# A decoder layer on one core: PSUM banks picked by waits already paid, and the last of four evictions waits for the other engine

## The reference

```
x = x + nystrom_attention(N(x))       # 16 heads of 16, 64 landmarks, softmax kernels q k_l, q_l k_l, q_l k
x = x + cross_attention(N(x), ctx)    # 64 context rows, masked softmax
x = x + ffn(N(x))                     # 8 experts, one picked per batch by its last token; N(x) + 0.3 (..)
```

```
KV = X @ V
V  = 0.25 * V @ (13 I - KV @ (15 I - KV @ (7 I - KV)))
```

## Time and profile before

| | |
|---|---|
| median of three runs | 1399.54 us |
| the profiled execution, its own time | 1397.8 us |
| span of that profile, first to last instruction | 1396.1 us |
| TensorE busy | 1355.2 us, 97% |
| VectorE, ScalarE, GpSimd busy | 1029.5, 667.0, 571.1 us |

### The profile page before, as it was taken

How to read it: one execution, slowest core, us unless ns; L and a number is a source line. 1 busy time by engine, 2 the same in 40 slices (tenths; PEclk the granted TensorE clock), 3 DMA queues, 4 the chain that set the end, 5 groups by cost and what they waited for, 6 DMA issues and landing times.

```text
span 1396.1 us, 53472 instructions
## 1 busy us (share of the span) xinstructions
PE 1355.2 (97%) x23732; PEld 889.7 (64%) x23732; DVE 1029.5 (74%) x2194; ACT 667.0 (48%) x1230; POOL 571.1 (41%) x799
## 2 busy tenths in 40 slices
PE   6998999999999999999999999999999999999998
PEld 4756666666766767665666766666666656676555
DVE  3487887758786886878778686877868777898641
ACT  2424355454555546355554644555454544435652
POOL 6223444443626244362534436153353543417132
PEclk9999999999999999999999999999999999999999
DMA  8002010120201011020101101010110100001122
GB/s 285 1 3 95 3 63 3 45 75 3 66 5 51 20 38 33 3 66 5 51 20 37 34 3 58 13 51 20 37 34 3 52 2 19 18 4 39 25 77 65
DMA packets 40536, 53.18 MB, mean 38 GB/s; under 512 B 9698, under 2 KB 30450, under 8 KB 40306
## 3 DMA queue, kind: packets, MB, share of 16 engines
q1 hardware_dynamic: 31602, 41.37, 9.2%
q10 hardware_dynamic: 8704, 8.39, 1.8%
HBM read 37.16 MB, written 12.59 MB: 36 GB/s over the span
## 4 chain that ended last, share of the span: by engine, by line
PE 85%; DVE 5%; ACT 3%; issue 2%; POOL 1%; DMA 1%; DVEq 1%; POOLq 0%; SPq 0%; ACTq 0%
PE bank L1322 41%; PE bank L1575 8%; PE bank L1341 7%; PE bank L1331 7%; PE bank L1564 3%; PE bank L1530 2%; PE bank L1418 2%; PE bank L1397 2%; PE bank L1462 2%; PE bank L1543 2%; PE bank L1451 2%; ACT p3T L896 1%; PE bank L1385 1%; PE bank L1562 1%; PE bank L1424 1%
## 5 line engine op out<-in xcount | busy, mean ns | idle before, releaser
L778 POOL TENSOR_TENSOR b<-ut,eye 128x256 f32<-128x256 f32 x192 | 137.6, 733 | 498.6 <-DVE ut L1161 428.9
L940 ACT ACTIVATE az<-bank 128x320 f32<-128x320 f32 x192 | 67.5, 400 | 185.6 <-PE bank L1331 185.2
L1322 PE MATMUL bank<-xnT_a,wqkv 128*128 128x512 f32 x256 | 123.6, 609 | 0.3 <-ACT xnT_a L864 0.3
L1218 DVE RECIPROCAL oT_x<-bank 128x256 f32<-128x256 f32 x64 | 109.2, 1733 | 19.2 <-PE bank L1575 19.2
L1322 PE MATMUL bank<-w2e,hT 128*128 128x256 f32 x512 | 119.0, 386 | 1.5 <-ACT hT L1006 1.4
L1218 DVE RECIPROCAL oT<-bank 128x256 f32<-128x256 f32 x64 | 111.5, 1747 | 10.6 <-PE bank L1575 10.6
L1322 PE MATMUL bank<-xnT_c,w1e 128*128 128x512 f32 x256 | 117.0, 597 | 1.3 <-DVE m_x L1192 0.9
L1090 DVE TENSOR_REDUCE m<-bank 128x1 f32<-128x512 f32 x128 | 82.9, 680 | 38.5 <-PE bank L1418 36.9
L1322 PEld LDWEIGHTS bank<-w2e,hT 128*128 128x128 f32 x512 | 96.0, 192 | 16.9 <-issue 2.7
L896 ACT ACTIVATE p3T<-bank 128x512 f32<-128x512 f32 x128 | 66.7, 603 | 79.1 <-PE bank L1451 78.9
L959 ACT ACTIVATE pT_x<-bank,neg_bias 128x512 f32<-128x512 f32 x128 | 79.9, 696 | 29.8 <-PE bank L1564 28.8
(11 more groups left out here) (223 smaller groups left out, 2979.2 us busy)
## 6 DMA issues: line engine op xcount, KB each, us to landing
x_in<-in_x SPq DMA_DIRECT2D x16, 512.0 KB, 3.8
w1e<-in_W SPq DMA_DIRECT2D x16, 512.0 KB, 3.5
w2e<-w2o SPq DMA_DIRECT2D x16, 512.0 KB, 4.1
out<-base ACTq DMA_DIRECT2D x32, 256.0 KB, 2.1
row_e<-w2o_row SPq DMA_DIRECT2D x16, 128.0 KB, 4.6
hT<-in_W2T SPq DMA_DIRECT2D x2, 512.0 KB, 6.5
pT_x<-in_ctxT SPq DMA_DIRECT2D x1, 1024.0 KB
ctxT<-in_ctxT SPq DMA_DIRECT2D x16, 64.0 KB, 2.6
```

Source lines behind the costliest of these rows:

```text
L778: return g.tensor_tensor(b7[:, q, :], ut[:, q, :], eye[28 if it else 7][:].unsqueeze(1) .broadcast_to([P, 4, LM]), ALU.subtract).then_inc( ...
L1218: return v.reciprocal(oT[x][:, k, cols], tile(i, ("den" + x, k))[:, cols]).then_inc(dve_done, 1)
L1322: last = mm(dst, lhsT, rhs, start=(k == 0), stop=(k == len(pairs) - 1))
```

## The change

Three things are changed; the written order, the arithmetic and the instructions that compute are the same.

First, `plan()` looks at the first three free banks and not at the first alone. It keeps, for A and for D, the highest number that TensorE has waited for. A bank costs 0 if its emptying step is covered by that already, 1 if the step is of an engine that this P step waits for anyway, and 2 otherwise. The cheapest is taken, the oldest of equal ones. A table `operands(step)` lists the A and D steps that a P step needs. Second, of the four evictions of an inverse level, the one that comes last in the written order first waits for both evictions of the other engine. Third, TensorE's waits are asked for together (`counts`): a wait is left out where another engine's step that is waited for has itself waited for it (`reached`), and the remaining ones are issued in an order fixed for each kind.

```diff
+    waited = {"A": 0, "D": 0}
     for engine, i, step in PROGRAM:
...
         if engine == "P":
+            asked = set()
+            for who, name in operands(step):
+                if done[who, i, name] > waited[who]:
+                    waited[who] = done[who, i, name]
+                    asked.add(who)
             for j in range(banks_of(step)):
-                bank[i, step, j], before[i, step, j] = free.pop(0)
+                price = [0 if emptier is None or done[emptier] <= waited[emptier[0]] else
+                         1 if emptier[0] in asked else 2 for _, emptier in free[:3]]
+                bank[i, step, j], emptier = free.pop(price.index(min(price)))
+                before[i, step, j] = emptier
+                if emptier and done[emptier] > waited[emptier[0]]:
+                    waited[emptier[0]] = done[emptier]
+                    asked.add(emptier[0])
...
+def closes_half(engine, i, step):
+    mine = ORDER[engine, i, step]
+    return all(ORDER[key] <= mine for h in range(2) for key in (("D", i, ("wb", step[1], h)), ("A", i, ("az", step[1], h))))
...
+        def counts(eng, emptied, i, **steps):
+            need = {"A": emptied["A"], "D": emptied["D"], "G": 0}
+            for who, names in steps.items():
+                need[who] = max([need[who], *[DONE[who, i, s] for s in names]])
+            mine = passed.setdefault(eng, {})
+            need = {who: n for who, n in need.items() if n > mine.get(done[who], 0)}
+            left = {who: n for who, n in need.items()
+                    if not any(reached[other, m].get(done[who], 0) >= n for other, m in need.items())}
+            for who, n in left.items():
+                for sem_, m in (*reached[who, n].items(), (done[who], n)):
+                    mine[sem_] = max(mine.get(sem_, 0), m)
+            return {who: left.get(who, 0) for who in need.keys() | set("ADG")}
...
 # ScalarE, before the eviction az
+                    if closes_half("A", i, step):
+                        if c := unmet(act, "D", i, ("wb", it, 0), ("wb", it, 1)):
+                            act.wait_ge(dve_done, c)
...
 # VectorE, before the eviction wb
+                    if closes_half("D", i, step):
+                        if c := unmet(dve, "A", i, ("az", it, 0), ("az", it, 1)):
+                            dve.wait_ge(act_done, c)
...
 # TensorE, one kind of many
                 elif kind in ("jT", "jZ"):
-                    if c := due(pe, "D", emptied, i, ("wb", it, 0), ("wb", it, 1)):
-                        pe.wait_ge(dve_done, c)
-                    if c := due(pe, "A", emptied, i, ("az", it, 0), ("az", it, 1)):
-                        pe.wait_ge(act_done, c)
+                    c = counts(pe, emptied, i, A=[("az", it, 0), ("az", it, 1)], D=[("wb", it, 0), ("wb", it, 1)])
+                    if c["D"]:
+                        pe.wait_ge(dve_done, c["D"])
+                    if c["A"]:
+                        pe.wait_ge(act_done, c["A"])
```

More of the change, by code:

```diff
@@ L327, with operands @@
 PROGRAM = program()
+def operands(step):
+    kind, n = step[0], step[1] if len(step) > 1 else 0
+    if kind in ("q", "k", "v"):
+        return [("A", ("xnTa", 0)), ("A", ("xnTa", 1))]
+    if kind in ("xnTb", "xnTc"):
+        return [] if step == ("xnTb", 0) else [("A", ("nmB",) if kind == "xnTb" else ("nmC", n))]
+    if kind in ("s3", "s1", "sx"):
+        return [("A", ({"s3": "k", "s1": "q", "sx": "qx"}[kind], n))]
+    if kind in ("t1", "tx"):
+        return [("A", ("mT" + kind[1],))]
+    if kind in ("x2T", "mT3", "t3", "mT1", "mTx"):
+        return [("D", ({"x2T": "soft2", "mT3": "mp3", "t3": "mT3", "mT1": "mp1", "mTx": "mpx"}[kind],))]
+    if kind in ("zT", "den1", "denx", "o1", "ox"):
+        e = {"z": "e3", "d": "e" + kind[-1], "o": "e" + kind[-1]}[kind[0]]
+        return [("A", (e, n, j)) for j in range(4)]
+    if kind in ("z", "a", "qx", "gate", "logit", "h", "y3"):
+        names = {"z": [("zT", 0), ("zT", 1)], "a": [("x2T",)], "qx": [("xnTb", 0), ("xnTb", 1)], "gate": [("xnTc", 1)],
+                 "logit": [("gate",)], "h": [("xnTc", 0), ("xnTc", 1)], "y3": [("h", f) for f in range(4)]}[kind]
+        return [("A", name) for name in names]
+    if kind in ("iT", "iZ"):
+        if n == 0:
+            return [("A", ("a", 0)), ("A", ("a", 1))]
+        return [("D", (x, n - 1, h)) for x in (("uz",) if kind == "iT" else ("uz", "ut")) for h in range(2)]
+    if kind in ("jT", "jZ"):
+        return [(e, (x, n, h)) for e, x in (("D", "wb"), ("A", "az")) for h in range(2)]
+    if kind == "y":
+        return [("D", ("uz", ITERS - 1, 0)), ("D", ("uz", ITERS - 1, 1))]
+    if kind in ("w1", "wx"):
+        return [("D", ("o" + kind[1], 0)), ("D", ("o" + kind[1], 1))]
+    return []
 def plan():
@@ L504, in unmet, with run @@
             return n if first(eng, done[who], n) else 0
-        def due(eng, who, emptied, i, *steps):
-            n = max(emptied[who], *[DONE[who, i, s] for s in steps])
-            return n if first(eng, done[who], n) else 0
+        def counts(eng, emptied, i, **steps):
+            need = {"A": emptied["A"], "D": emptied["D"], "G": 0}
+            for who, names in steps.items():
+                need[who] = max([need[who], *[DONE[who, i, s] for s in names]])
+            mine = passed.setdefault(eng, {})
+            need = {who: n for who, n in need.items() if n > mine.get(done[who], 0)}
[5 more added lines that the diff above has]
+            return {who: left.get(who, 0) for who in need.keys() | set("ADG")}
         def tile(i, step, j=0):
             return banks[BANK[i, step, j]]
-        def run(who, body):
+        def run(who, eng, body):
             for engine, i, step in PROGRAM:
@@ L517, in run @@
                     body(i, step)
+                    if (who, i, step) in DONE:
+                        reached[who, DONE[who, i, step]] = dict(passed.get(eng, {}))
         def half(n):
@@ L1013, in body @@
                     return last.then_inc(act_done, 1)
-            run("A", body)
+            run("A", act, body)
         @block.vector
@@ L1374, in body @@
                         pe.wait_ge(ctx_loaded, 16 * (i + 1))
+                    c = counts(pe, emptied, i)
+                    if c["A"]:
+                        pe.wait_ge(act_done, c["A"])
+                    if c["D"]:
+                        pe.wait_ge(dve_done, c["D"])
                     for r in range(2):
@@ L1387, in body @@
                     x = kind[-1]
[L1388 to L1392, removed]
-                            pe.wait_ge(act_done, c)
+                    c = counts(pe, emptied, i, **({"G": [("lnB", 0)]} if (x, n) == ("b", 0) else {"A": [("nmB",) if x == "b" else ("nmC", n)]}))
+                    if c["D"]:
+                        pe.wait_ge(dve_done, c["D"])
+                    if c["A"]:
+                        pe.wait_ge(act_done, c["A"])
+                    if c["G"]:
+                        pe.wait_ge(pool_done, c["G"])
                     for k in range(KD):
@@ L1453, in body @@
                 elif kind == "zT":
[L1454 to L1457, removed]
+                    c = counts(pe, emptied, i, A=[("e3", n, j) for j in range(4)], D=[("v", 0), ("v", 1)])
+                    if c["D"]:
+                        pe.wait_ge(dve_done, c["D"])
+                    if c["A"]:
+                        pe.wait_ge(act_done, c["A"])
                     for h in range(2):
@@ L1605, in body @@
                         pe.wait_ge(expert_out_loaded, 32 * (i + 1))
-                    if c := due(pe, "A", emptied, i, *[("h", f) for f in range(FM)]):
-                        pe.wait_ge(act_done, c)
+                    c = counts(pe, emptied, i, A=[("h", f) for f in range(FM)])
+                    if c["D"]:
+                        pe.wait_ge(dve_done, c["D"])
+                    if c["A"]:
+                        pe.wait_ge(act_done, c["A"])
                     for t in range(2):
@@ L1620, in body @@
                     fuse_consts(pe)
+                    c = counts(pe, emptied, i)
+                    if c["A"]:
+                        pe.wait_ge(act_done, c["A"])
+                    if c["D"]:
+                        pe.wait_ge(dve_done, c["D"])
                     last = chain(o[0:EXPERTS, 0:D], [(b2T[:, k, :], wfo[:, k, :]) for k in range(KD)])
                 last.then_inc(pe_done, 1)
-            run("P", body)
+            run("P", pe, body)
 def kernel(**inputs):
```

242 lines of the change are left out of this document (149 added, 93 removed), and 3 rows, old and new, of the table OPERANDS_FROM.

## The result

The changed kernel took 1428.06 us (median of five executions, 1424.85 to 1431.53) against 1399.49 before: 28.6 us or 2.0% slower, ratio 1.0204 with a 95% interval of 1.0184 to 1.0224. A sixth execution, of 3806.4 us, was in a slow state and is left out; with it the median is 1428.89. Forecast were 1427 us in a range of 1409 to 1440. The profiled execution after took 1431.53 us with a span of 1429.8, so 33.7 us more span than before.

The account below looks back on a forecast made before the run. TensorE, 97% busy in a fixed order, was taken as the bound. Delays of 0.11 + 0.40 + 0.42 + 0.63 + 0.18 = 1.74 us a turn, times 16, gave 27.8 us and 1427 us; range 1409 to 1440.

Parts of the forecast that it names:

- middle turn: One repeat of the regular pattern, nine in all (batches 4 to 12); predicted 1.74 us later each.
- s1.1: TensorE step whose new bank is emptied by a ScalarE step ending at 710.28; predicted +0.11 us.
- iT.1: TensorE step at inverse level 1 whose new bank waits for VectorE's reciprocal of the batch before; predicted +0.40 us.
- jT.1: TensorE step at inverse level 1, behind a ScalarE eviction now held for VectorE's last one; predicted +0.42 us.
- t1.1: TensorE step whose new bank waits for ScalarE's first eviction of level 2, one step later; predicted +0.63 us.
- jZ.5: TensorE step at inverse level 5, behind a ScalarE eviction held for VectorE's; predicted +0.18 us.
- jT.2: TensorE step at inverse level 2; predicted no longer to wait for VectorE's eviction, with the turn's shift staying nonetheless.
- The single wait at level 0: One wait instead of two before TensorE's step there; up to 0.09 us earlier, not counted in the sum.
- `a`: TensorE step taking a bank emptied by the gelu of the same stretch; counted as nothing, behind later ScalarE work.
- ragged turns: The other seven batches, with other orders; the same 1.74 us each taken as an estimate, possibly nothing or twice that.
- Met waits are free: On TensorE, 230 fewer waits (1473 to 1243) put at nothing, being dealt with while earlier matmuls run.
- The rival that dropping them would make it 1388: Waits cost TensorE time even when met: 230 x 0.051 = 11.7 us less; chance 0.06.

Follow-up runs that it names:

- the banks alone: The changed kernel without the held evictions; the new choice of banks and the dropped waits stay: 1418.97 us, ratio 1.0138 to the kernel before.
- the counts alone: The changed kernel with banks handed out oldest first and no held evictions, leaving only the new counting of TensorE's waits: 1395.69 us, ratio 0.9975 to the kernel before.
- the level 4 hold alone: The changed kernel with banks handed out oldest first and evictions held at level 4 only: 1397.95 us, ratio 0.9999 to the kernel before.

## Why the prediction was right

- **PE is the bound and each late step adds.** Right: 1.57 us per middle turn for 1.74 worked out, and the parts measured alone add up to the whole, 29.3 to 28.6 us.
- **The steps**, by their starts against the step before, in most middle turns: s1.1 +0.11 (0.11 predicted), iT.1 +0.40 (0.40), jT.1 +0.42 (0.42), t1.1 +0.63 (0.63), jZ.5 +0.16 (0.18). jT.2 starts 0.18 sooner after t1.1 and den1.1 waits 0.18 longer, so in most turns the shift stays, as argued.
- **What made 1.57 of 1.74** are mostly two things put at nothing. In every fourth turn jT.2 starts 0.46 sooner and den1.1 gives back only 0.20, so in the mean 0.09 of t1.1's 0.63 is hidden. The single wait at level 0 moved jT.0 up, by 0.07 us in the mean, and iT.1 did not eat this in full. `a` was late by 0.21 us, and xnTb.1 behind it gave 0.19 back: 0.09 is the cover that was named, for the banks alone show as much, and the rest is the new counting, which moves xnTb.1 up without the banks too. The banks alone thus lose 0.12 at `a`, which the prediction put at nothing.
- **Holds and banks.** 9.0 us for the holds (16 x 0.60 = 9.6 predicted) and 23.3 for the banks (18.2). In a middle turn they are 0.44 and 1.12 (0.60 and 1.14). So the holds were over-sized in the middle. In the seven ragged turns the banks were under-sized, (23.3 - 9 x 1.12) / 7 = 1.9 a turn, or 1.5 from the 20.4 us at one clock.
- **The ragged turns** were the estimate, 7 x 1.74 = 12.2. The profile has 33.7 - 9 x 1.57 = 19.6 outside the nine middle turns, up to 6 of it clock; by the timed difference it is 28.6 - 14.1 = 14.5. This is the term furthest off; the 1.74 that was too high in nine turns made up for part of it, so that the sum came within about 1 us of the time is in part luck.
- **An open wait's price.** A wait on the weight load releases PE 0.05 us after the eviction in these rows (0.06 taken). A held eviction starts 0.04 after the other engine's end.
- **Met waits are free.** Right for their number: 1.7 ns each where they stand behind. Wrong as a general rule: 2400 of them ahead of the steps' own waits cost 28 us. The count was a little off: the old order has 1482 waits and not 1473, so 239 went. The rival that dropping them would make it 1388 fell; the counts alone, with 37 waits fewer, gained 3 us, most of it clock. The Trainium skill, Advanced Engine Details and Errata, section Miscellaneous Facts (Network/Comms), has 50 to 100 ns for reading a semaphore from a sequencer. The 51 ns that a wait instruction lasts here agree with the lower figure as a length; what one cost PE was 1.7 ns where other work stood in front.
- **A turn of 83.5 us** came, but of its 1.57 more only 1.15 to 1.4 are idle PE (1.68 a turn, where it was 0.26 to 0.54); busy time rose from 81.5 to 81.8 at a clock of 1.00, with the same matmuls in a turn. Why it rose is open; no run tested it.

## What to carry to other kernels

In an engine that runs at 97% in a fixed order, count a wait by how late its producer is, not by how many waits there are: a met wait behind a step's own waits was worth 2 ns here and an open one up to 0.63 us in every turn. When a resource is picked to save a wait, take only one whose release has been waited past already; a younger release of "an engine that is waited for anyway" is a longer wait. Where two waits stand at one step, issue the one that ends last first, and look at what another step on the same engine empties before moving anything ahead of it.

## What the runs showed of the hardware

- After stops of PE the granted clock can be half: 6.8 us at 0.50 behind a stop of 2.24 us, 3.4 us behind one of 2.33 at the same step in the kernel before. Not every stop did it; with the level 4 hold alone, a stop of 2.1 us at 1149.5 left the clock at 1.00. Between executions of the changed kernel with a mean clock of 1.000 and of 0.994 the time differs by 6.7 us, so versions some 3 us apart are to be compared at one clock.
- The first issued wait of a PE step and its later ones differ by 0.09 us from the producer's end to the matmul: 0.05 or 0.06 against 0.14 or 0.15. Turning the two round moved the starts by 0.05 to 0.07.
- 2400 wait instructions of 51 ns, 122 us by their lengths, cost 4 us of time when they stand behind the step's real waits, and 28 us ahead of them.
